# Earlier bias rows, another split of the indirect stores, and three output pieces added onto a copy of x

## The reference

```python
xn = layernorm(x)
# attention branch, per sequence
q, v = xn @ Wq, xn @ Wv
state[t] = sigmoid(beta) * state[t-1] + v[t]         # per head
y = layernorm(q * state) * ln_g + ln_b
s = (y * silu(xn @ Wg)) @ Wo
# expert branch
logits = xn @ router.T                                # 8 experts
gates, idx = softmax(top2(logits))
f = sum over the two experts e: gate_e * (silu(a_e) * b_e) @ w_out[e].T   # a_e, b_e: halves of xn @ w_in[e].T
g = silu(f + bias)
return x + s * g
```

## Time and profile before

| | us |
|---|---|
| three runs | 524.05, 522.06, 522.58 (median 522.58) |
| profiled execution | 521.35 |
| its span, first to last instruction | 519.6 |
| PE busy in the span | 429.3 (83%) |
| DVE, ACT, POOL busy | 305.8 (59%), 214.3 (41%), 273.5 (53%) |

### The profile page before, as it was taken

One profiled execution on the slowest core, in us unless ns is written; L12 is line 12 of the kernel. 1 busy time (PEld: TensorE's weight loads), 2 busy tenths in 40 slices (PEclk: granted clock), 3 DMA queues, 4 the chain that ended last, 5 costly groups with the idle time before them and its releaser, 6 DMA issues.

```text
span 519.6 us, 11882 instructions
## 1 busy us (share of the span) xinstructions
PE 429.3 (83%) x3446; PEld 337.6 (65%) x3447; DVE 305.8 (59%) x589; ACT 214.3 (41%) x340; POOL 273.5 (53%) x524
## 2 busy tenths in 40 slices
PE   1767879977965899999999999999999999998000
PEld 1643446544534798888898888888888888765000
DVE  4898999949973534545444545454545454444077
ACT  4871276775752732423242433242433333232050
POOL 4712777877785034646464655465555656543200
PEclk9998999998978999999999999999999999999655
DMA  8950229998622134566334433343434343442498
GB/s 254 315 161 22 83 71 335 321 356 279 221 86 92 43 92 88 118 149 102 62 51 71 61 61 53 69 61 61 61 61 64 65 59 57 70 59 29 75 340 301
DMA packets 52693, 64.70 MB, mean 125 GB/s; under 512 B 5552, under 2 KB 47536, under 8 KB 52656
## 3 DMA queue, kind: packets, MB, share of 16 engines
q1 hardware_dynamic: 37712, 45.55, 28.6%
q0 software_dynamic: 13296, 17.83, 20.9%
q10 hardware_dynamic: 1664, 1.06, 0.7%
HBM read 40.02 MB, written 28.74 MB: 132 GB/s over the span
## 4 chain that ended last, share of the span: by engine, by line
PE 48%; DMA 14%; DVE 14%; issue 11%; POOL 7%; SPq 2%; ACT 1%; another core or an unknown queue 1%; POOLq 0%; DVEq 0%; ACTq 0%
PE bankC L1086 16%; PE bankB L1086 15%; PE bankA L1086 13%; DMA y_dram<-rows_raw 8%; POOL slots_dram L470 4%; PE bankD L1210 3%; DMA rows_raw<-slots_dram 2%; DMA w_raw<-x_in 2%; DVE w_raw L1064 1%; POOL stat L434 1%; DVE work L931 1%; DMA w_raw<-y_dram 1%; DVE work L981 1%; DVE bn L756 1%
## 5 line engine op out<-in xcount | busy, mean ns | idle before, releaser
L544 POOL DMA_INDIRECT y_dram<-rows_raw x71 | 113.3, 1595 | 31.7 <-issue 31.7
L1086 PE MATMUL bankC<-w_raw,rows_raw 128*128 x852 | 99.5, 273 | 2.0 <-DVE rows_raw L1056 2.0
L1086 PEld LDWEIGHTS bankC<-w_raw,rows_raw 128*128 128x128 f16 x852 | 82.0, 98 | 13.6 <-issue 2.6
L470 POOL DMA_INDIRECT slots_dram<-rows_raw,pos_i x64 | 69.5, 1086 | 39.2 <-issue 20.8
L1086 PE MATMUL bankA<-rows_raw,w_raw 128*128 128x256 f16 x768 | 90.0, 274 | 0.0
L1086 PE MATMUL bankB<-rows_raw,w_raw 128*128 128x256 f16 x768 | 89.1, 273 | 0.0
L1086 PEld LDWEIGHTS bankA<-rows_raw,w_raw 128*128 x768 | 75.5, 98 | 9.4 <-issue 0.2
L1086 PEld LDWEIGHTS bankB<-rows_raw,w_raw 128*128 x768 | 75.2, 98 | 8.3
L1003 DVE TENSOR_TENSOR rows_raw<-rows_raw 128x512 f16<-128x512 f32 x64 | 44.3, 692 | 45.6 <-ACT rows_raw L695 45.6
L999 DVE SCALAR_TENSOR_TENSOR rows_raw<-rows_raw,bankA 128x512 f32<-128x512 f32 x32 | 22.0, 687 | 73.4 <-ACT rows_raw L690 73.4
L695 ACT ACTIVATE rows_raw<-rows_raw 128x512 f16<-128x512 f32 x64 | 40.3, 629 | 49.6 <-DVE rows_raw L999 49.6
(11 more groups left out here) (182 smaller groups left out, 655.1 us busy)
## 6 DMA issues: line engine op xcount, KB each, us to landing
rows_raw<-slots_dram SPq DMA_DIRECT2D x32, 260.0 KB
work<-w_exp_in SPq DMA_DIRECT2D x16, 512.0 KB
w_raw<-x_in SPq DMA_DIRECT2D x9, 512.0 KB, 4.6
w_raw<-w_exp_in SPq DMA_DIRECT2D x8, 512.0 KB, 7.8
y_dram<-bias_in SPq DMA_DIRECT2D x4, 1024.0 KB
w_raw<-y_dram SPq DMA_DIRECT2D x8, 512.0 KB, 7.5
out<-w_raw SPq DMA_DIRECT2D x8, 512.0 KB, 3.7
work<-x_in SPq DMA_DIRECT2D x7, 512.0 KB
```

What stands on the lines that cost most here:

```text
L470: pool.indirect_dma_start(out=slots_dram, out_offset=bass.IndirectOffsetOnAxis(slot, 0), in_=row, in_offset=None, bounds_check=SLOTS - 1, ...
L544: pool.indirect_dma_start(out=y_dram, out_offset=bass.IndirectOffsetOnAxis(to, 0), in_=ys[i][:, s, :], in_offset=None, bounds_check=ROWS_O ...
L1086: last = pe.matmul(out_ap, lhsT, rhs, start=(n == 0), stop=(n == len(todo) - 1))
```

## The change

Three things change, none of them in the loop over the expert blocks.

1. SP writes the bias rows into `y_dram` behind group 0 of the expert weights, no longer behind group 4.
2. GpSimd waits for the router's eighth product before its first indirect store, no longer for VectorE's second `choose`. Behind the eight first stores it issues 9, 10, 8, 8, 8, 8 and 5 in rounds 0 to 6, no longer 8 in each. The store number 32 still waits for `place(1)`, and the first for `place(0)`.
3. For the first three chunks SP copies x to the output, DRAM to DRAM, behind the last slot load. In the tail VectorE only multiplies them by s, and GpSimd adds them onto the output with one DMA each (accumulating, 512 KB). The other five are stored as before.

```diff
-SCATTERS_EACH = 8
+SCATTERS_CHUNK = (9, 10, 8, 8, 8, 8, 5, 0)
@@ SP, head
-            for group in range(3):
+            load_w(0)
+            for t in range(0, NT, 2 * TPC):
+                sp.dma_start(y_v[:, t:t + 2 * TPC, :], bias.unsqueeze(1).to_broadcast([P, 2 * TPC, D]))\
+                  .then_inc(y_started, 16)
+            sp.dma_start(y_v[:, NT, :], bias).then_inc(y_started, 16)
+            for group in range(1, 3):
                 load_w(group)
@@ SP, behind groups 3 and 4
-            for t in range(0, NT, 2 * TPC):
-                sp.dma_start(y_v[:, t:t + 2 * TPC, :], bias.unsqueeze(1).to_broadcast([P, 2 * TPC, D]))\
-                  .then_inc(y_started, 16)
-            sp.dma_start(y_v[:, NT, :], bias).then_inc(y_started, 16)
@@ SP, behind the last slot load
+            for c in range(ADDING):
+                tiles = slice(c * TPC, (c + 1) * TPC)
+                sp.dma_start(out_v[:, tiles, :], x_v[:, tiles, :]).then_inc(x_placed, 16)
             sp.wait_ge(y_ps, BLOCKS)
@@ SP, tail
-            for c in range(CH):
-                sp.wait_ge(dve_added, c + 1)
+            for c in range(ADDING, CH):
+                sp.wait_ge(dve_added, c - ADDING + 1)
                 sp.dma_start(out_v[:, c * TPC:(c + 1) * TPC, :], res[c]).then_inc(stored, 16)
-            sp.wait_ge(stored, 16 * CH)
+            sp.wait_ge(stored, 16 * (CH - ADDING))
+            sp.wait_ge(added, 16 * ADDING)
@@ GpSimd, stage of the slot stores
-            pool.wait_ge(chosen_ready, GROUPS)
+            pool.wait_ge(logits_done, CH)
@@
-                end = min(done + SCATTERS_EACH, N_SCATTERS)
+                end = done + SCATTERS_CHUNK[c]
@@ GpSimd, behind the last scatter
+            pool.wait_ge(x_placed, 16 * ADDING)
+            for c in range(ADDING):
+                pool.wait_ge(gated, c + 1)
+                pool.dma_start(out_v[:, c * TPC:(c + 1) * TPC, :], res[c], accum_op=ALU.add)\
+                    .then_inc(added, 16)
@@ VectorE, tail
                 finish(c)
-                if c >= 1:
+                if c >= ADDING + 1:
                     add_x(c - 1)
```

More of the change, by code:

```diff
@@ L65 @@
 GC = CH // GROUPS
+ADDING = 3
 WSCALE = 16.0
@@ L71 @@
 SCATTERS_FIRST = 8
-SCATTERS_EACH = 8
+SCATTERS_CHUNK = (9, 10, 8, 8, 8, 8, 5, 0)
+assert SCATTERS_FIRST + sum(SCATTERS_CHUNK) == N_SCATTERS
 def repeat(eng, peeled, end, stride, body):
@@ L304, in build @@
         moe_silu, gated, dve_added = map(sem, ("moe_silu", "gated", "dve_added"))
-        stored = sem("stored")
+        stored, added, x_placed = sem("stored"), sem("added"), sem("x_placed")
         x_v = x.rearrange("(t p) d -> p t d", p=P)
```

## The result

| | before | changed |
|---|---|---|
| median, us | 522.67 (522.06 to 524.09, 5 runs) | 526.81 (526.10 to 527.50, 5 runs) |
| ratio to before | | 1.0073, 95% interval 1.0057 to 1.0089 |
| profiled execution, us | 521.35 | 526.81 |
| its span, us | 519.6 | 525.0 |

The change makes the kernel 0.7% slower. That is inside the range of the prediction, but it is not the likeliest case, "no change" at 523.4. The two spans differ by 5.4 us, and three places of the trace account for it: the last pair block's gate on VectorE comes 1.1 us earlier (442.74 for 443.86), from there to the first y load it takes 3.7 us more (51.88 for 48.14: the ladder), and from that load to the end 2.8 more (30.4 for 27.6: the tail).

What follows compares the result with a forecast made beforehand. Bounds: GpSimd's slot stores to 160 us, TensorE from 165 to 450, then chained scatters and a tail limited by DMA and VectorE. -3.3 - 0.9 + 0 + 0.9 + 4.1 = +0.8 us: median 523.4, range 518 to 527.5.

Steps and rivals of the forecast that it cites:

- last slot store: End of GpSimd's indirect-store stage: fewer stores behind the seventh variance bring it 3.3 us earlier, or 1.3 if idle time stays.
- clock step: TensorE's first 24 expert products: with the gap before them down to 0.8 us, the lower clock goes, -0.9 us.
- bias rows in the head: Early weight loading: bias traffic moved there costs 0, bounds 0 and +4.1 us.
- copy beside the ladder: Late chain of adding scatters: one or two share DMA engines with the copy of x, +0.9 us, upper bound +3.6.
- adding pieces in the tail: Final load-to-store stretch: three added pieces cost more DMA work than plain stores, +4.1 us, bounds -2.3 and +7.3.
- First scatters earlier: Start of the slot stores: first eight end near 54 us instead of 58.8; alone worth 0, it buys room.
- 9, 10, 8, ...: Slot-store rounds: later variances shift, five stores instead of eight follow the seventh; last store 3.3 us earlier.
- Round-robin: Tail: DMA engines alternate between queues, additions hold up y loads, last y piece near 515.5 us; +4.7 instead of +4.1.
- the additions ride free: Rival, tail: additions overlap with plain transfers, tail -2.3, sum -6.0, 516.6 us; chance 0.22.
- the stall moves into the head: Rival, early stretch: an engine waits 4.1 us between 20 and 47 us, sum +4.9, 527.5 us; chance 0.10.
- The additions cost more: Rival, tail: an added row costs 135 ns, tail +7.3, sum +4.0, 526.6 us; chance 0.16.
- The new split does nothing: Rival, slot-store stage: the recurrence, fed 2.56 us late, becomes the bound; sum about +4, 526.6 us; chance 0.07.

Runs made afterwards that it cites:

- the split by nines: Kernel before with bias rows moved behind group 0 and stores 9, 8, 8, 8, 8, 8, 7 in rounds 0 to 6, nothing added: 521.25 us, ratio 0.9967.
- The kernel with ten first stores: Kernel before with bias rows moved, ten stores before the first variance, then 9, 8, 8, 8, 8, 8, 5, nothing added: 518.87 us, ratio 0.9902.
- the kernel with the early copy: Changed kernel with the copy of x issued behind group 5 of the expert weights instead of the last slot load: 522.43 us, ratio 0.9998.

## Why the prediction was right or wrong

Its terms, in us:

| term | forecast | measured |
|---|---|---|
| last slot store | -3.3 | -0.95 |
| clock step | -0.9 | -0.9 (3.71 to 2.79), by another cause |
| bias rows in the head | 0 | 0 |
| copy beside the ladder | +0.9 | +3.7 |
| adding pieces in the tail | +4.1 | +2.8 |

The first two terms together reach the end of the expert loop as -1.1 (forecast -4.2). With +3.7 and +2.8 that is the +5.4 between the two spans, where +0.8 was forecast. The time is inside the range because the range was wide, and because the tail came 1.3 us cheaper than forecast; the two other errors, 3.1 and 2.8 us, are in the same direction.

- *First scatters earlier* was right: the first variance starts at 57.54 (forecast 57.7), the second at 72.76 (72.87).
- *9, 10, 8, ... is where the first term failed.* The starts were forecast at 104.1, 118.7 and 147.2 and came at 104.60, 119.85 and 149.36, the last store at 159.53 for 157.2. I carried the variances' durations over from the rounds of before. But they depend on when GpSimd comes to them: late, they meet the conversions and take up to 4.40 us. The "3.0 us of lag" that I counted as free room is what moves them there. The 2.01 us of idle time did go, but it was an accident of the profiled execution, which the other kernels with the bias rows in their old place don't show; against the one whose stage is that of before (160.21) the last store gains 0.7. The working's "-1.3 if the idle time stays" was nearest.
- *Clock step*: the number was right by luck. I closed the gap with slots that come 3.3 us earlier; they come 0.44 earlier, and the gap is closed by the recurrence, which ends 3.06 us later. In the traces here TensorE takes 3.7 to 5.2 us for its first 24 products where it idled 2.3 to 6.0 before the slots, and 2.79 where it idled at most 1.0. This is also where the split's own gain is seen (1.2 us there, 1.4 against the split by nines), not in its stores. The kernel with ten first stores shows the price from the other side (3.41 us idle, then 4.20 us).
- *The copy* was mis-sized: +0.9 for +3.7, at the upper bound of +3.6. I priced packets that take turns, 8 x 0.055 us for each of two scatters. One scatter was hit, and it lost 1.9 us before its first packet and 1.6 between its packets, where 8 turns of 0.055 us make 0.44. A ladder step is mostly latency (3.8 us, of which the packets' time is 1.35), so the thing to price was what full engines do to a chain of waits. The Trainium skill's rule (DMA: Bandwidth & Descriptors, Latency and other measured facts), 2 us for an access to HBM under high load, gave +3.6 as the sum of two scatters with 1.8 us each. The trace agrees with that sum, 3.7, but not with its parts: one scatter pays 3.6 and none 1.8. Whether the mechanism is that access is not shown.
- *The additions:* the size of a packet was right (forecast 102 ns, measured 101), so was the surcharge (5.7 us of work, measured 5.9, though against packets of 40 ns and not 45) and the slack (1.6; 5.9 - 4.0 = 1.9 by that surcharge). What I left out is the 1.0 us that the tail wins when VectorE has three operations less: with plain stores by GpSimd it is 26.69 us against 27.7 in the kernel without the adding part. The end comes 3.8 us behind VectorE's last addition there as in the kernel before, and that addition 0.9 us earlier than before, counted from the first y load. 4.0 - 1.0 = 3.0, measured 2.8 to 3.0. I had treated VectorE's gain as either all of the result or none of it. GpSimd's issue of a piece, taken as 1.6 to 6.4 us, is 1.34 (4.02 for three).
- *Round-robin* (the Trainium skill, DMA: Bandwidth & Descriptors, Queues, rings and completion order): the trace agrees in that both queues get the same number of packets, 233 to 232, and in that the last y piece is late: its silu starts at 512.27, 3.1 us behind that of before counted from the first y load. By the estimate it would have landed some 9 us late, and the forecast from it, 4.7, was worse than the plain sum, since the additions' first packets came only at 506.7 us, not at 500.6.

Of the rivals, *the additions ride free* and *the stall moves into the head* are refuted. *The additions cost more* gave the right time, 526.6, by a wrong term, which is luck: the packets cost 101 ns, not 135. *The new split does nothing* gave the same time and named the right mechanism in part: a recurrence that is fed late. The split does bring 2 us, though, as its own run shows, and the late recurrence is no loss to it.

## What to carry to other kernels

Price a change of schedule between two engines not only by start times: look whether the same instruction has different durations in the rows, and what the other engine does in the long ones; here taking two small instructions a round from GpSimd was worth some 6 us (ratio 0.9785 for 0.9902), more than any order of its stores. A copy beside a chain of small dependent DMAs cost 3.7 us by what it delayed, not by the engine time it shared, and nothing that could be measured where no such chain ran. A DMA that adds took 61 ns more for each KB than GpSimd's plain store: three saved vector operations did not pay for that in a tail where the DMA engines were the other limit. And a wait has two ends: before a gap is counted as closed by what comes earlier, look what may end later on its other side.

## What the hardware showed that I had not expected

- A GpSimd instruction of 0.24 us takes up to 1.07 us, one of 1.04 us 1.87 (2.09 once in the kernel before), while VectorE runs 1.15 us instructions with two SBUF inputs; beside a write of zeros they take 0.23 and 1.04.
- Three adding DMAs of 512 rows were issued from 501.57 us on, and their first packet came at 506.7: 5.1 us. In the kernel with the early copy too: issue at 496.89, no packet until 502.0. It is not the addition: with plain stores the issue is at 498.84 and the first packet at 503.5.
- GpSimd's plain stores of the same pieces have packets of 4 KB at 150 ns, the adding ones of 1 KB at 101 ns: 40 ns for 1 KB against 101.
- An adding scatter beside a DRAM to DRAM copy that fills the engines took 7.32 us for 3.6 to 4.1, with its first packet 4.0 us after its issue for 2.1.
- The 24 products behind a gap of 6.03 us took 4.58 us at a granted clock of 0.50; behind one of 0.21 us, at 1.00, they took 2.79.
